# A conditioned stack of four layers on one core: the loops over chunks written out as straight code

## The reference

```
x = x + g * Attention(modulate(layernorm(x)))            # layer 0: 16 heads of 64
x = x + g * W2(gelu(W1(modulate(layernorm(x)))))         #          hidden 1024
x = x + g * Attention(modulate(rmsnorm(x)), rope)        # layer 1: 16 heads of 16, q and k normed
x = x + g * W2(silu(W1 h) * (W3 h))                      #          hidden 682, padded to 768
x = x + g * Attention(modulate(layernorm(x)), rope)      # layer 2: 16 heads of 16
x = x + g * W2(gelu(W1(...)));  x = x + Wo(gelu(V x) * tanh(G x))   # and a gated unit
x = x + low-rank product whose factors come from the condition      # layer 3
```

## Time and profile before

| what | value |
|---|---|
| median of three executions | 2127.19 us (2124.84 to 2128.36) |
| the profiled execution's own time | 2128.56 us |
| its span, first to last instruction | 2126.8 us |
| mean granted clock of TensorE | 0.96 of full |
| PE busy | 1911.8 us, 90% of the span |
| DVE, ACT, POOL busy | 1319.5, 994.4, 787.6 us |
| DMA queue q8, kind "instruction" | 132 packets, 2.16 MB |

### The profile page before, as it was taken

The page is one execution under the profiler, slowest core; times in us unless marked ns, Lnnn a source line. Parts: engine busy times, 40 slices in busy tenths (PEclk is TensorE's granted clock), DMA queues, the critical chain, the costliest instruction groups (busy, mean ns, idle before and its releaser), DMA issues. The chain is left out here.

```text
span 2126.8 us, 44677 instructions
## 1 busy us (share of the span) xinstructions
PE 1911.8 (90%) x17318; PEld 1485.0 (70%) x17318; DVE 1319.5 (62%) x2028; ACT 994.4 (47%) x1693; POOL 787.6 (37%) x737
## 2 busy tenths in 40 slices
PE   5999999999979998688988899969999799988898
PEld 4777777777867776466766777747777677766675
DVE  4454555555554555588898577768888555544455
ACT  3433433443336666365666344324555466643222
POOL 1220211121123334566677333456878533340000
PEclk8999999999999999799999999979999899999999
DMA  5100000000010000100000000010000000003222
GB/s 184 70 2 2 2 2 2 2 2 2 2 41 21 0 0 1 45 2 3 2 2 2 27 0 0 0 41 2 2 0 2 27 5 0 0 21 103 75 70 80
DMA packets 26300, 44.73 MB, mean 21 GB/s; under 512 B 4240, under 2 KB 12240, under 8 KB 26000
## 3 DMA queue, kind: packets, MB, share of 16 engines
q1 hardware_dynamic: 24848, 42.01, 6.0%
q10 hardware_dynamic: 1280, 0.23, 0.1%
HBM read 35.94 MB, written 6.29 MB: 20 GB/s over the span
## 5 line engine op out<-in xcount | busy, mean ns | idle before, releaser
L1205 DVE TENSOR_TENSOR Glb<-Gfb,Ghb 128x512 fp32r<-128x512 f32 x176 | 165.2, 948 | 97.6 <-ACT Ghb L1156 95.9
L443 PE MATMUL bank<-HH,W1b 128*128 128x512 f32 x448 | 184.9, 413 | 16.1 <-PEq L1511 7.1
L325 POOL TENSOR_TENSOR Tm<-Dv,MOD 128x512 f32<-128x512 f32 x94 | 108.4, 1173 | 236.9 <-DVE Dv L382 159.1
L444 PE MATMUL bank<-HL,W1b 128*128 128x512 f32 x448 | 177.3, 396 | 0.0
L445 PE MATMUL bank<-HH,W1b 128*128 128x512 f32 x448 | 177.2, 396 | 0.0
L443 PE MATMUL O<-Ghb,W2b 128*128 128x512 f32 x352 | 142.9, 406 | 37.1 <-DVE Glb L1205 37.0
L463 POOL TENSOR_TENSOR spare<-RT 128x1 f32<-128x1 f32 x32 | 6.4, 201 | 401.1 <-DVE RT L454 401.1
L314 POOL TENSOR_TENSOR XS<-Tm 128x512 f32<-128x512 f32 x48 | 69.8, 1454 | 219.1 <-ACT Tm L280 214.2
L445 PE MATMUL O<-Ghb,W2b 128*128 128x512 f32 x352 | 138.0, 392 | 0.0
L444 PE MATMUL O<-Glb,W2b 128*128 128x512 f32 x352 | 137.8, 391 | 0.0
L1386 PE MATMUL bank<-WQKa,HH 128*128 128x512 f32 x256 | 91.6, 441 | 38.8 <-DVE HL L390 16.6
(11 more groups left out here) (262 smaller groups left out, 5161.6 us busy)
## 6 DMA issues: line engine op xcount, KB each, us to landing
w<-l_w_dram SPq DMA_DIRECT2D x33, 256.0 KB, 3.4
X<-xT_dram SPq DMA_DIRECT2D x16, 256.0 KB, 6.7
out_dram<-XO SPq DMA_DIRECT2D x8, 512.0 KB, 2.7
wm<-w_mods_dram SPq DMA_DIRECT2D x4, 768.0 KB, 5.1
W2b_f<-l_w_dram SPq DMA_DIRECT2D x11, 256.0 KB, 5.5
WQK_f<-l_wqk_dram SPq DMA_DIRECT2D x8, 256.0 KB, 8.6
W1b_0f<-l_w_dram SPq DMA_DIRECT2D x8, 256.0 KB, 3.7
wm<-w_mods_dram SPq DMA_DIRECT2D x4, 384.0 KB, 6.3
```

Source lines behind the costliest of these rows:

```text
L325: nc.gpsimd.tensor_tensor(Tm[:, k].rearrange("p (b t) -> p b t", t=T), Dv[:, k].rearrange("p (b t) -> p b t", t=T), m, ALU.mult).then_inc( ...
L443: nc.tensor.matmul(out, w_lo_ap, x_hi, start=first, stop=False)
L444: nc.tensor.matmul(out, w_hi_ap, x_lo, start=False, stop=False)
L1205: nc.vector.tensor_tensor(Gl[m % gb][:], gf, Gh[m % gb][:].bitcast(F32), ALU.subtract).then_inc(g_lo.h, 1)
```

## The change

`chunks` and `steps` lose their loops. Both call the body with Python integers, c = 0 to 7, and the argument `more` takes the values it had (2 for chunks 0 to 5, then 1, then 0). The calls lose the engine argument. Nothing else is edited.

```diff
-        def chunks(eng, body, unrolled=False):
-
-            if unrolled:
-                for c in range(NCH):
-                    body(c, c % 2, 2 if c < NCH - 2 else NCH - 1 - c)
-                return
-            with eng.Fori(0, NCH // 2 - 1) as j:
-                body(2 * j, 0, 2)
-                body(2 * j + 1, 1, 2)
-            body(NCH - 2, 0, 1)
-            body(NCH - 1, 1, 0)
+        def chunks(body):
+
+            for c in range(NCH):
+                body(c, c % 2, 2 if c < NCH - 2 else NCH - 1 - c)
...
-                        chunks(pe, steps(step, lambda c: None))
+                        chunks(steps(step, lambda c: None))
...
-                        chunks(act, body, gate)
+                        chunks(body)
...
-                def steps(eng, step):
+                def steps(step):
...
-                    body(0, 0, 2)
-                    with eng.Fori(0, NCH // 2 - 2) as j:
-                        body(2 * j + 1, 1, 2)
-                        body(2 * j + 2, 0, 2)
-                    body(NCH - 3, 1, 2)
-                    body(NCH - 2, 0, 1)
-                    body(NCH - 1, 1, 0)
+                    for c in range(NCH):
+                        body(c, c % 2, 2 if c < NCH - 2 else NCH - 1 - c)
```

More of the change, by code:

```diff
@@ L871, in _ @@
                         step(0, 1, 0, 2, first=True)
-                        chunks(act, steps(step, lambda c: None))
+                        chunks(steps(step, lambda c: None))
                     @block.vector
@@ L979, in _ @@
                         dve.wait_ge(x_in[2].h, x_in[2].at(16 * DH * (NCH - 2)))
-                        chunks(dve, steps(step, residual))
+                        chunks(steps(step, residual))
                         step_v.pending = step_c.n[0]
@@ L1010, in body @@
                             residual_pool(pool, c)
-                        chunks(pool, body)
+                        chunks(body)
                 d_in.passed(16 * n_small); step_v.passed(step_v.pending)
@@ L1140, in body @@
                                     f.pe_mean(pe, cc)
-                        chunks(pe, body, gate)
+                        chunks(body)
                     @block.scalar
@@ L1242, in body @@
                                 residual_dve(dve, c, l, G_M, bcol_out, O2)
-                        chunks(dve, body, gate)
+                        chunks(body)
                     @block.gpsimd
@@ L1626, in _ @@
                         step(0, 0, 0, 2, first=True)
-                        steps(pe, step)
+                        steps(step)
                         out_t(pe, NT - 1)
@@ L1694, in _ @@
                         step(0, 0, 0, 2, first=True)
-                        steps(act, step)
+                        steps(step)
                         oh(NT - 1, 1)
@@ L1772, in _ @@
                         fr.dve_norm(dve, 1)
-                        steps(dve, step)
+                        steps(step)
                         for tt in (NT - 2, NT - 1):
@@ L1808, in _ @@
                         step(0, 0, 0, 2, first=True)
-                        steps(pool, step)
+                        steps(step)
                         add(NCH - 1, 1)
```

## The result

The median of four executions after is 2100.60 us (2097.81 to 2105.32), that of four executions before on the same chip 2127.65. The ratio is 0.9878, 95% interval 0.9857 to 0.9898: a gain of 26 us (22 to 30). The forecast was 14 us, 2113.2 with a range of 2109.0 to 2119.0. So the sign held, and the size and the range did not. The profiled execution took 2100.56 us.

A forecast was written before the change was run, and what follows sets the result against it. PE was taken as the bound, busy 1911.8 of 2126.8 us, losing time where it idles or runs at low clock. Gains of 9.71 + 3.16 + 1.10 = 13.97 us led to 2113.2 us, range 2109.0 to 2119.0.

The forecast's parts named there:

- Returns on PE: PE's loop returns go: 9.71 us gained in A0, 3.16 in A1, nothing for the other seven.
- the low clock behind A0's returns: After A0's two returns PE runs at a lower clock; 4.48 of A0's 9.71 us.
- where the body is still held: A return is free if the loop's instructions are still held; PE waits if they must be read again; no separate size.
- the rule that it takes from the Trainium skill: Branches outside the current two-page window wait for a fetch; seven more stalls, 20.6 us more gain; given no chance.
- The table loads: Six of 61 ACT loads go, at loop heads in B0, B1, B2; only B1's two gain, 1.10 us.
- Register instructions: Semaphore values and addresses no longer computed in loops on PE, DVE, ACT, POOL; taken as 0, at most 1.9 us.
- Fetching: Straight code brings 19 more instruction packets in A2, B0, B1, B2; cost taken as 0, upper end 47.5 us.
- Larger gain: Register work counts in A1 and its clock stays up: 1.9 us more gain, 2111.3 us; chance 0.12.
- Only A0's part: Only A0's 9.71 us arrives; a different phase between engines eats 4.26 us in A1 and B1: 2117.5 us; chance 0.09.
- Nothing: PE's stalls are no property of the returns and come again: time stays at 2126 us; chance 0.04.
- slower: Added packets come late on PE in B0, B1, B2, A2, 2.50 us idle each, up to 2160.7 us; chance 0.05.

The follow-up runs named there:

- only_pe: The kernel before with PE's code alone straight in all six blocks, the other engines keeping their loops: 2119.29 us against 2127.46, ratio 0.9964.
- only_act: The kernel before with ACT's code alone straight in all six blocks, the other engines keeping their loops: 2120.06 us against 2127.46, ratio 0.9963.
- shift64: The kernel before, all loops kept, with 64 more semaphore instructions at the head of PE's stream: 2131.69 us against 2124.55.
- e4_behind: The kernel after with a semaphore increment on ACT before the first two pieces' Gelu or Silu, putting the table load behind the waits again: 2109.72 us against 2100.60.
- only_dve: The kernel before with DVE's code alone straight in all six blocks, the other engines keeping their loops: 2124.56 us against 2127.46, ratio 0.9983.
- shift176: The kernel before, all loops kept, with 176 more semaphore instructions at the head of PE's stream: 2157.69 us, 1.60% slower.
- e5_ahead: The kernel before, loops kept, with ACT's table load written ahead of the wait in B0, B1 and B2: 2122.19 us against 2127.46, ratio 0.9973.

## Why the prediction was wrong

- **Returns on PE: the mechanism was right, the size too large.** The two stalls in A0 and the one in A1 went with PE's loop, and the seven others cost nothing. Forecast for all was 12.87 us; only_pe, with PE's code alone straight, gained 8.2 (interval 4.7 to 10.4). The mis-sized term is the low clock behind A0's returns. The prediction took 4.48 us for it from one trace, in which the two chunks ran at 0.95 and 0.98. In five other traces with the same loops they ran at 0.98 and 1.00 (only_act), and the two returns together cost 6.4 to 6.9 us in place of 9.71. The idle part, 5.23, came back in all of them within 0.4 us. Also, the reason for telling costly returns from free ones, "where the body is still held", lacked that this hangs on the start of the loop; shift64 takes A1's stall away without touching A1. The forecast counted on all instances as they were, and the change removed all, so this cost nothing here. The price that the prediction gives for the rule that it takes from the Trainium skill (20.6 us more) is too high even by that rule: B0's, B1's and B2's bodies are 1.7 to 1.9 blocks, which a window of two pages can hold.
- **The table loads: the step that failed.** The prediction weighed only the six loads that go, 1.10 us, and held "DVE's multiply and split and so PE's second product wait for that Silu" without asking what the load waits for. The 55 that stay were never costed. The row was there: the load at 1231.95 is released by PE's bank after 4.40 us of idle, though a load needs nothing from PE. What stays behind a wait in before stands ahead of it after. e4_behind puts it at 9.1 us by the medians (7.5 by the feed-forward blocks), at a forecast of 0. Of the 12.9 us gained in those blocks, 5.0 lie in B1's five middle chunks, 6.0 at the three heads, and 2.0 in the middle chunks of B0 and B2. Of the 6.0 at the heads e4_behind gives back 3.6; what made the other 2.4 is open.
- **Register instructions: taken at 0, bound 1.9; too low, a second step that failed.** The middle chunks give 0.20 x 10 = 2.0 us in B0 and B2, and 1.9 in A2's five (164.9 to 162.9). A0's, without the returns, give 0.7. That is 4.6 us before B1 and A1. The error was in the comparison of a straight chunk with loop chunks, 32.96 against 32.89. The window of 32.96 starts at 1585.29, before the loop is over: PE leaves it at 1590.19, ACT at 1592.78, DVE at 1593.17 and POOL at 1595.53. Cut from residual to residual, the last full stretch of the loop and the first in which every engine is out of it, in the trace of before, and the same straight stretch after:

```profile
1543.65:1576.57 32.92, 31.59 (x375) 24.28 (x375) 29.32 (x48) 17.46 (x33) 25.48 (x24) 1.00 0.00 0
1609.26:1641.95 32.69, 31.52 (x375) 24.37 (x374) 29.11 (x48) 18.82 (x37) 26.45 (x24) 1.00 0.01 2
...
1581.94:1614.60 32.66, 31.50 (x375) 24.37 (x374) 29.10 (x48) 18.82 (x37) 26.44 (x24) 1.00 0.01 2
```

  So the trace of before had the 0.23 us a chunk, had the window been put behind the loop. In B0, where only_dve shows DVE's 0.19 us a chunk, both windows of the prediction were of the loop.
- **Fetching: right in that it costs nothing.** 8 packets more, where 19 were expected: by block A2 has 6 more and B0, B1 and B2 3 each, but A0 has 5 and A1 2 fewer, which the prediction held unchanged. No "issue" stall comes from them: B0's chunks are at 26.11 while its code is brought in.
- **Rivals.** "Larger gain" was the right side with the wrong cause and a seventh of the size. "Only A0's part" had the phase between engines eat A1's and B1's gain; the chunks without a stall in A1 and B1 show that it ate neither. "Nothing" and "slower" did not come.
- **The range** ended at 2109.0, because every bound came from windows that both contained the load behind its wait. No bound was taken from "all of ACT's loads move", though the order of instructions after the change shows the wait on the other side of the load. The margins of 2.3 and 1.5 us at its ends are not the 1.8 that the text gives; neither matters at a miss of 8.
- **The sum by what the runs showed**, an estimate: 8.2 for the returns, 9.1 for the place of the loads, up to 1.1 for the six that go, 4.6 for register instructions, together 23 of the 26 (22 to 30) us. Two of the four terms were at 0 in the forecast. That the forecast missed by 12 us and not by 17 is the oversized return's doing, which is luck.
- **Left open:** most of the 8 us between the engines' sum and the whole; how much is POOL's, in A2 above all; 4 us of shift64; and 2 to 3 us in any one block, which the clock moves about.

## What to carry to other kernels

When values that instructions wait for turn from registers into constants, look at where each wait lands: a register instruction between two waits carried the first of them ahead of an ACT table load, and without it that wait is on the ACTIVATE behind the load. A load that the profile shows as released by PE's bank is a load that could have been done already. It can be had in a loop too, by writing the load ahead of the wait. Before a straight chunk is taken as the measure of straight code, see that its window begins after every engine has left the loop. Don't take a free return as a property of the loop, and don't price a return from one trace: the idle is steady, the clock behind it is not.

## What the runs showed of the hardware

- PE's branch back to a loop head takes 207 to 247 ns or 3.3 to 4.8 us, with nothing between; the same loop of 6.3 blocks of 256 instructions does either, by what stands ahead of it. Behind long ones the granted clock falls (0.91 over A2's chunk in shift176, which took 5.9 us more; 0.98 and 1.00 over A0's two in only_act, 4.3 and 2.6 us more).
- An ACT table load takes 1283 ns, and the function behind it starts 0.01 us after its end where nothing else is waited for (before, B0). A load with idle time to stand in costs a chunk nothing: in e5_ahead B1's chunk with a second load takes 25.49 us and the one without it 25.61, and after, B1's PE is busy for 25.15 of 25.15 us.
- A semaphore increment on PE took 153 ns in a row of them at the program's start. Two register instructions of DVE's sequencer between the end of PE's matmul and DVE's residual made the residual start 0.24 us after it in place of 0.04 (before and only_dve, B0).
